# Four copies of the sums, a last block of one pair of bins per step, and a bias taken as a maximum, in a graph kernel

## The chip, the cores and the metric

The kernel runs on one core of a Trainium2 chip. Its time is that of one execution on the device, in microseconds (us), as the median of several runs. The core has five engines with a queue of instructions each, which run in order and wait for each other by semaphores: TensorE (PE in the rows; PEld is its weight load), VectorE (DVE), ScalarE (ACT), GpSimd (POOL) and SyncE (SP, which here only issues DMAs). Sixteen DMA engines move the data.

## The reference, cut to what matters

N = 6250 nodes of 64 values, E = 206250 edges sorted by `dst`, 64 values per edge:

```python
h = jnp.maximum(_layernorm(x), 0.0)                    # per node
m = jnp.concatenate([h[dst], edge_attr], axis=1)       # per edge
m = jax.nn.relu(m @ W1.T + b1)                         # 128 wide
m = jax.nn.relu(m @ W2.T + b2)                         # 128 wide
agg = segment_sum(m, src) / jnp.maximum(cnt, 1.0)      # by source node
z = jax.nn.relu(concatenate([h, agg, u[0]]) @ Wa.T + ba)
out = x + z @ Wb.T + bb
```

The edges come in the order of `dst`, the sums go by `src`, which lies at random. Everything is float32.

## The kernel before, in words

The edges are cut into 403 groups of 512 (four tiles of 128). The main loop has one step per group, and each engine runs the same steps from its own program; in step s PE works on group s in the first layer, on s-1 in the second and on s-2 in the sums.

The first layer of a group is one matmul (L1168) of 128x512: 64 rows are edge values, 64 select the projected node (`R`, built on DVE at L955 from the row `dstR` that SP broadcasts, and `L`, a window of the node table). ACT applies Relu (L821). The second layer is four matmuls (L1183) on top of one bf16 matmul (L1181) that puts b2 into the bank; ACT's Relu (L828) writes `h2`.

There are two ways to add a group's rows up by source. In a *plain* group (226 of them) DVE builds four masks of equal sources (L986), PE adds rows of the same source (L1157), ACT copies the result (L814), and POOL adds it to `sums` in memory by four indirect DMAs (L732). There are three copies of `sums` (NSETS), taken in turn; within one copy a scatter waits until the one before has landed. ACT's copy has four buffers, and waits for the landings of the group four plain ones before.

In a *sorted* group (177: the odd ones from 3 to 379, without every 24th from 95 on) DVE ranks the edges within 49 bins of source (L962, L964, L967), PE permutes the rows into slots, four per bin and 32 spare ones (L1133, two tiles ahead of the second layer and two behind), ACT copies them (L804), and SP stores them (L519). The spare ones are read back (L525), added by source with a mask (L974, PE L1194, ACT `vscat` L837, whose result also waits for an earlier landing) and scattered by POOL once (L720). The slots are collected by blocks of 30 sorted groups: for each of 25 pairs of bins, a *unit*, SP reads the block's rows (L536), DVE builds masks (L1016), PE adds (L1144, eight matmuls, 16 passes in the records), and DVE adds to `acc` in SBUF (L943). The reads have two buffers: unit m waits for unit m-2. Units of a block are spread over the steps of the next block; those of the last block, after the last sorted group, come two per step in steps 387 to 399, one behind the first layer and one at the step's end.

After the loop 13 chunks of rows follow: SP reads three copies, DVE adds them and `acc` (L1030 to L1032), divides by the count (L1035, L1036, L1039), PE transposes and applies the two last layers, and SP stores.

The order of work on an engine is only the order of the code in its `step`. Steps 0 to 4 of SP also write the zeros of the third copy (ZAFTER).

Of the kernel before, what the change touches and what calls it, by code (L numbers as in the profile page):

```python
# [5 lines left out]
P = 128  # L6
TILE = 128
# [22 lines left out]
NSETS = 3  # L30
ZQ = 5
ZFIRST, ZMID = 9, 2
ZAFTER = (0, 1, 1, 1, 1)
# [14 lines left out]
LAST_SORTED = 380  # L48
SKIP_FROM, SKIP = 72, 24
# [8 lines left out]
BLOCK = 30  # L58
# [11 lines left out]
def is_sorted(g):  # L70
    return 2 < g < LAST_SORTED and g % 2 == 1 and not (g >= SKIP_FROM and g % SKIP == SKIP - 1)

# [49 lines left out]
def mid_unit(s):  # L122
    return UNITS_AT[s][:-1] if s in UNITS_AT else []


def end_unit(s):
    return UNITS_AT[s][-1:] if s in UNITS_AT else []
# [12 lines left out]
assert NBIN == BA * BA and PACK * BA <= P and NS % (4 * PACK) == 0 and max(len(u) for u in UNITS_AT.values()) <= 2  # L140


def build(nc, x, src_cols, dst_cols, src_rows, dst_rows, ea, u, w1t, b1, w2t, b2, wat, ba, wbt, bb, out):
# [13 lines left out]
    with ctx:  # L157
# [64 lines left out]
        s1 = take(KC)  # L222
# [72 lines left out]
        rc = sb("rc", [P, 2, RCH], f32)  # L295
# [5 lines left out]
        psVsum = bank[:, 7, 2 * W:2 * W + C]  # L301
# [257 lines left out]
        def _(pool):  # L559
# [64 lines left out]
            whole(G.tensor_copy(b2p[:, 0, :], b2b[:, :]))  # L624
            whole(G.tensor_tensor(b2w[:, 0, :], b2b[:, :], b2p[:, 0, :], ALU.subtract))
            whole(G.tensor_copy(b2p[:, 1, :], b2w[:, 0, :]))
            whole(G.tensor_tensor(b2w[:, 1, :], b2w[:, 0, :], b2p[:, 1, :], ALU.subtract))
            whole(G.tensor_copy(b2p[:, 2, :], b2w[:, 1, :]))
            for k in range(3):
                whole(G.tensor_scalar(b2w[:, k % 2, :] if k < 2 else b2b[:, :], b2p[:, k, :], ident[:, k:k + 1], None, ALU.mult))  # L630
            whole(G.tensor_tensor(b2w[:, 0, :], b2w[:, 0, :], b2w[:, 1, :], ALU.add))
            whole(G.tensor_tensor(b2w[:, 0, :], b2w[:, 0, :], b2b[:, :], ALU.add))
            G.tensor_copy(b2R[:, :, :], b2w[:, 0, :].unsqueeze(1).broadcast_to([P, TPG, H])).then_inc(b2_ready, 1)
# [115 lines left out]
        def _(act):  # L749
# [46 lines left out]
            def evac_slots(g, t):  # L796

                n = BINNED_NO[g]
                act.wait_ge(slot_done, TPG * n + t + 1)
                if t == 3 and is_sorted(g + 2 - VSUM):  # L800
                    act.wait_ge(vsum_done, BINNED_NO[g + 2 - VSUM] + 1)
                if t == 0:
                    wait(act, slot_out[n % 2], 32 * (n // 2))
                nc.scalar.activation(slot_sb[:, n % 2, :, t, :], psSlot(t), ACT.Copy).then_inc(slot_ready, 1)  # L804

            for s in range(STEPS):
                g = s - 2
# [10 lines left out]
                if s < NG:  # L818
                    act.wait_ge(l1_done, s + 1)
                    wait(act, l2_done, s - 1)  # L820
                    nc.scalar.activation(h1[:, s % 2, :], psL1(s % 2), ACT.Relu).then_inc(h1_ready, 1)  # L821
                g = s - 1
                if 0 <= g < NG:
                    summed(act, g - 2)
                    if is_sorted(g):
                        nc.scalar.activation(h2[:, g % 2, :, C], srcF[:, TPG * g:TPG * (g + 1)], ACT.Copy).then_inc(key_ready, 1)
                    act.wait_ge(l2_done, g + 1)
                    nc.scalar.activation(h2[:, g % 2, :, 0:H], psL2(g % 2).rearrange("p (t f) -> p t f", t=TPG), ACT.Relu).then_inc(h2_ready, 1)  # L828
                if is_sorted(s - 2):
                    evac_slots(s - 2, 2)  # L830
                    evac_slots(s - 2, 3)
                if is_sorted(s - VSUM):
                    n = BINNED_NO[s - VSUM]
                    act.wait_ge(vsum_done, n + 1)
                    if n >= 2:
                        landed(act, BINNED[n - 2], 0)
                    nc.scalar.activation(vscat[:, n % 2, :], psVsum, ACT.Copy).then_inc(vscat_ready, 1)  # L837

            for c in range(NCH + 2):
                if c < NCH:  # L840
                    act.wait_ge(aggT_psum, c + 1)
# [4 lines left out]
                    nc.scalar.activation(aggT[:, c % 2, 0:w], bank[:, c % 2, 0:w], ACT.Copy).then_inc(aggT_ready, 1)  # L846
# [10 lines left out]
        def _(dve):  # L857
# [69 lines left out]
            dve.wait_ge(toscrap_ready, 1)  # L927
            dve.wait_ge(binF_ready, 1)
# [16 lines left out]
            for s in range(-3, STEPS + 1):  # L945
# [73 lines left out]
                if s == XBB_STEP:  # L1019
                    dve.wait_ge(wz_in, 16 * 8)  # L1020
# [3 lines left out]
            for c in range(NCH + 3):  # L1024
                if c < NCH:
# [4 lines left out]
                    link(VE.tensor_tensor(s1[:, 0:m * C], SA[:, s, 0, 0:m * C], SA[:, s, 1, 0:m * C], ALU.add))  # L1030
                    link(VE.tensor_tensor(s2[:, 0:m * C], s1[:, 0:m * C], SA[:, s, 2, 0:m * C], ALU.add))
# [3 lines left out]
                    link(VE.tensor_scalar(rc[:, 0, 0:m], s1v[:, :, H], 1.0, None, ALU.max))  # L1035
# [3 lines left out]
                    VE.tensor_tensor(agg[:, c % 2, 0:m, :], s1v[:, :, 0:H], rc[:, 1, 0:m].unsqueeze(2).broadcast_to([P, m, H]), ALU.mult).then_inc(agg_ready, 1)  # L1039
# [10 lines left out]
        def _(pe):  # L1050
# [58 lines left out]
            def free_last(s):  # L1109

                wait(pe, vscat_ready, sum(1 for g in BINNED if g <= s - VSUM - 1))

            def bin_tile(g, t, general):

                n = BINNED_NO[g]
                if t == 0:
# [5 lines left out]
                    free_last(g + 2)  # L1122
# [25 lines left out]
            def step(s, general):  # L1148
                g = s - 2
                if is_plain(g):  # L1150
                    n = PLAIN_NO[g]
                    pe.wait_ge(h2_ready, g + 1)
                    pe.wait_ge(mask_ready, n + 1)
                    free_sums(g - 1)
                    free_last(s)
                    for t in range(TPG):
                        last = T.matmul(bank[:, 6 + t // 2, (t % 2) * C:(t % 2 + 1) * C], S[:, n % 4, t, :], h2[:, g % 2, t, 0:C], start=True, stop=True)  # L1157
                    last.then_inc(sum_done, 1)
                if is_sorted(g):
                    bin_tile(g, 0, general)  # L1160
                    bin_tile(g, 1, general)
# [13 lines left out]
                for k, q in mid_unit(s):  # L1175
                    add_up(k, q, general)
                g = s - 1
                if 0 <= g < NG:
                    pe.wait_ge(h1_ready, g + 1)
                    wait(pe, h2_ready, g - 1)  # L1180
                    T.matmul(psL2(g % 2), onesb[:, :], b2R[:, :, :].rearrange("p t f -> p (t f)"), start=True, stop=False)  # L1181
                    for t in range(TPG):
                        last = T.matmul(psL2(g % 2)[:, t * H:(t + 1) * H], h1[:, g % 2, t * TILE:(t + 1) * TILE], w2[:, :], start=False, stop=t == TPG - 1)  # L1183
# [4 lines left out]
                if is_sorted(s - VSUM):  # L1188
                    n = BINNED_NO[s - VSUM]
                    pe.wait_ge(vmask_ready, n + 1)  # L1190
                    if not is_sorted(s - 2):
                        free_sums(min(s - 2, NG - 1))
                        free_last(s)
                    T.matmul(psVsum, vS[:, n % 2, :] if not general else zeros[:, 0:P], V[:, n % 2, 0:C], start=True, stop=True).then_inc(vsum_done, 1)  # L1194
# [19 lines left out]
                for k, q in end_unit(s):  # L1214
# [93 lines left out]
```

## Time and profile before

| | us |
|---|---|
| median of 3 runs (lowest, highest) | 2417.41 (2416.22, 2422.64) |
| profiled execution | 2404.49 |
| its span, first to last instruction | 2402.7 |
| busy: PE, DVE, ACT, POOL | 1894.7, 1289.1, 954.8, 1764.7 |
| mean granted clock of TensorE | 0.934 of full |
| DMA moved | 395.44 MB, 165 GB/s on average |

The profile is of one execution. Busy shares are averages over stages with different limits. A row of waits tells how long an engine stood idle before a line, and which event ended it; "issue" means that nothing in the profile was waited for. The chain of waits is followed back from the last instruction.

### The profile page before, as it was taken

What the parts mean: (1) busy time and instruction counts of PE and PEld (TensorE: products, weight loads), DVE (VectorE), ACT (ScalarE), POOL (GpSimd) and SP (SyncE); (2) the same over time, 40 slices, a digit from 0 to 9 for tenths busy, and PEclk for the clock granted to TensorE, in tenths of its full rate; (3) what the DMA queues carried; (4) which work ended last, traced back from release to release, by engine and by line L of the source; (5) the groups of instructions that cost most, each with busy time, mean ns of one, the idle gap of its engine ahead of it and who ended that gap; (6) DMA issues with size and microseconds to landing.
All of it is one profiled execution on the core that took longest, in us unless ns stands there. A gap on an engine that the chain in (4) does not pass through costs nothing.

```text
span 2402.7 us, 44999 instructions
## 1 busy us (share of the span) xinstructions
PE 1894.7 (79%) x12635; PEld 1565.7 (65%) x12840; DVE 1289.1 (54%) x4867; ACT 954.8 (40%) x2147; POOL 1764.7 (73%) x1131
## 2 busy tenths in 40 slices
PE   3788888888888888888888888888888879754546
PEld 2566666767766676767676677767677767553544
DVE  8655545555555555646555555555555656423227
ACT  2355544444434443444443444444443434311112
POOL 8477887777787777778777778787777777774370
PEclk8899999999999999999999999999999999876788
DMA  7688888988888888988888888988888889764446
GB/s 286 151 159 164 160 147 176 179 184 166 178 156 175 170 174 170 179 162 167 173 183 170 169 167 166 182 170 170 172 177 167 176 176 179 145 101 96 88 65 191
DMA packets 392057, 395.44 MB, mean 165 GB/s; under 512 B 51262, under 2 KB 296158, under 8 KB 391302
## 3 DMA queue, kind: packets, MB, share of 16 engines
q1 hardware_dynamic: 235030, 319.95, 48.3%
q0 software_dynamic: 155664, 71.47, 33.2%
q8 instruction: 113, 1.85, 0.3%
q10 hardware_dynamic: 1120, 1.11, 0.2%
q14 instruction: 130, 1.06, 0.2%
HBM read 221.11 MB, written 171.21 MB: 163 GB/s over the span
## 4 chain that ended last, share of the span: by engine, by line
POOL 33%; DMA 31%; issue 16%; PE 13%; DVE 4%; SPq 1%; ACT 1%; POOLq 0%; DVEq 0%; ACTq 0%
POOL sums L732 28%; DMA sums<-regA,idx 20%; DMA sums<-vscat,vidx 9%; POOL sums L720 4%; PE bank L1144 4%; PE bank L1183 3%; PE bank L1168 2%; PE bank L1157 2%; PE bank L1133 2%; DMA src<-rows_src 1%; DMA regC<-slots 1%; ACT h L828 1%; DVE regC L906 1%; DVE regC L986 1%; DVE regC L912 0%
## 5 line engine op out<-in xcount | busy, mean ns | idle before, releaser
L732 POOL DMA_INDIRECT sums<-regA,idx x904 | 1430.5, 1582 | 494.9 <-issue 232.5
L1183 PEld LDWEIGHTS bank<-w,h 128*128 128x128 f32 x3224 | 442.0, 199 | 151.4 <-issue 138.4
L1133 PE MATMUL bank<-h,regC 128*128 128x130 f32 x2832 | 397.4, 284 | 128.8 <-ACT h L828 128.8
L1133 PEld LDWEIGHTS bank<-h,regC 128*128 128x128 f32 x2832 | 352.6, 195 | 151.6 <-ACT h L828 151.6
L1183 PE MATMUL bank<-w,h 128*128 128x128 f32 x3224 | 439.7, 281 | 14.0 <-issue 4.2
L1168 PE MATMUL bank<-regA,L 128*128 128x512 f32 x806 | 435.4, 624 | 2.0 <-DVE regA L955 2.0
L1157 PE MATMUL bank<-h,regC 128*128 128x129 f32 x1808 | 260.0, 288 | 165.8 <-ACT vscat L837 135.0
L1144 PE MATMUL bank<-regC 120*128 120x129 f32 (+1 forms) x2352 | 314.6, 290 | 92.7 <-DVE regB L943 92.7
L828 ACT ACTIVATE h<-bank 128x512 f32<-128x512 f32 x403 | 241.1, 598 | 330.2 <-PE bank L1183 328.3
L804 ACT ACTIVATE regC<-bank 128x260 f32<-128x260 f32 x708 | 272.7, 386 | 244.3 <-PE bank L1133 187.5
L1144 PEld LDWEIGHTS bank<-regC 120*128 120x128 f32 (+1 forms) x2352 | 294.4, 203 | 104.1 <-issue 102.6
L1157 PEld LDWEIGHTS bank<-h,regC 128*128 128x128 f32 x1808 | 226.4, 196 | 200.3 <-issue 170.1
L720 POOL DMA_INDIRECT sums<-vscat,vidx x177 | 280.0, 1582 | 76.7 <-issue 43.6
L962 DVE TENSOR_REDUCE rank<-bank 128x4 f32<-128x196 f32 x177 | 64.1, 362 | 498.9 <-PE bank L1207 497.6
L814 ACT ACTIVATE regA<-bank 128x516 f32<-128x516 f32 x226 | 135.6, 600 | 492.3 <-PE bank L1157 245.1
L821 ACT ACTIVATE h<-bank 128x512 f32<-128x512 f32 x403 | 240.4, 597 | 151.7 <-PE bank L1168 150.4
L986 DVE SCALAR_TENSOR_TENSOR regC<-src,srcF,tri 128x128 f32<-128x128 uint16 x904 | 266.3, 350 | 18.1 <-DMA src<-rows_src 11.6
L1016 DVE SCALAR_TENSOR_TENSOR regC<-regC,lows 120x512 f32<-120x512 f32 (+1 forms) x294 | 189.8, 686 | 89.9 <-DMA regC<-slots 89.6
L955 DVE TENSOR_SCALAR regA<-dstR,oh_row 64x512 f32<-64x512 bf16 x403 | 205.5, 510 | 29.6 <-DMA dstR<-rows_dst 17.4
L949 DVE TENSOR_TENSOR regC<-bank,overs 128x128 f32<-128x128 f32 x177 | 51.5, 291 | 295.7 <-PE bank L1213 291.2
L964 DVE TENSOR_TENSOR regC<-bank,ranks 128x784 f32<-128x784 f32 x177 | 172.4, 974 | 5.6
L1168 PEld LDWEIGHTS bank<-regA,L 128*128 128x128 f32 x806 | 127.5, 199 | 3.1 <-DVE regA L955 2.9
(140 smaller groups left out, 1339.2 us busy)
## 6 DMA issues: line engine op xcount, KB each, us to landing
regC<-slots SPq DMA_DIRECT2D x245, 243.8 KB
regA<-in_ea SPq DMA_DIRECT2D x202, 256.0 KB
slots<-regC SPq DMA_DIRECT2D x177, 260.0 KB
slots<-regC SPq DMA_DIRECT2D x177, 203.1 KB
src<-rows_src SPq DMA_DIRECT2D x226, 128.0 KB
dstR<-rows_dst SPq DMA_DIRECT2D x403, 64.0 KB
sums<-regA,idx POOLq DMA_INDIRECT x904
L<-p_table SPq DMA_DIRECT2D x403, 32.0 KB
```

What stands on the lines that cost most here:

```text
L720: nc.gpsimd.indirect_dma_start(out=sums[k], out_offset=bass.IndirectOffsetOnAxis(ap=vidx[:, n % 4:n % 4 + 1], axis=0), in_=vscat[:, n % 2, ...
L732: nc.gpsimd.indirect_dma_start(out=sums[k], out_offset=bass.IndirectOffsetOnAxis(ap=idx[:, n % RING, t:t + 1], axis=0), in_=scat[:, n % 4, ...
L804: nc.scalar.activation(slot_sb[:, n % 2, :, t, :], psSlot(t), ACT.Copy).then_inc(slot_ready, 1)
L821: nc.scalar.activation(h1[:, s % 2, :], psL1(s % 2), ACT.Relu).then_inc(h1_ready, 1)
L828: nc.scalar.activation(h2[:, g % 2, :, 0:H], psL2(g % 2).rearrange("p (t f) -> p t f", t=TPG), ACT.Relu).then_inc(h2_ready, 1)
L955: VE.tensor_scalar(R[D:P, g % RING, :], dB[D:P, g % 4, :], oh_row[D:P, :], None, ALU.is_equal).then_inc(oh_ready, 1)
L986: mask = VE.scalar_tensor_tensor(out=S[:, n % 4, t, :], in0=sB[:, n % 4, t * TILE:(t + 1) * TILE], scalar=srcF[:, TPG * g + t:TPG * g + t ...
L1133: last = T.matmul(psSlot(t)[:, k, :], place, h2[:, g % 2, t, :], start=True, stop=True)
L1144: last = T.matmul(psUnit[:, i * C:(i + 1) * C], oh2[0:rows, m % 2, i, t, :] if not general else zeros[0:rows, 0:LO], BR[0:rows, m % UNIT_R ...
L1157: last = T.matmul(bank[:, 6 + t // 2, (t % 2) * C:(t % 2 + 1) * C], S[:, n % 4, t, :], h2[:, g % 2, t, 0:C], start=True, stop=True)
L1168: T.matmul(psL1(s % 2), L[:, s % RING, :], R[:, s % RING, :], start=True, stop=True).then_inc(l1_done, 1)
L1183: last = T.matmul(psL2(g % 2)[:, t * H:(t + 1) * H], h1[:, g % 2, t * TILE:(t + 1) * TILE], w2[:, :], start=False, stop=t == TPG - 1)
```

## The change

There are four copies of `sums`, so that a scatter waits for the landing of the fourth before it; the zeros of the fourth copy are written in steps 5 to 7 of SP. All odd groups from 3 to 367 are sorted (183), none is skipped, and groups 368 to 402 are all plain; blocks have 31 sorted groups. Units come in even steps, at most one per step, always at the end of PE's step; those of the last block one per step in steps 376 to 400. PE and ACT do the first layer ahead of the sums. The second layer's matmul of b2 is gone: DVE writes max(W2 h1, -b2) into `h2`, which is relu(W2 h1 + b2) - b2, and b2 is added behind the mean, in ACT's evacuation of the transposed mean (with Relu, and a term that keeps nodes without edges at 0). POOL only negates b2. The sum of the spare slots moves from bank 7 to bank 1 (that of the units) and behind the ranks in PE's step, so `free_last` goes.

```diff
-NSETS = 3
+NSETS = 4
-ZAFTER = (0, 1, 1, 1, 1)
+ZAFTER = (0, 1, 1, 1, 1, 1, 2, 2)
-LAST_SORTED = 380
-SKIP_FROM, SKIP = 72, 24
+LAST_SORTED = 368
-BLOCK = 30
+BLOCK = 31
 def unit_steps():
-    firsts = [block[-1] + VREAD + 1 for block in BLOCKS]
+    firsts = [block[-1] + VREAD + 2 for block in BLOCKS]
...
-            s = firsts[k] + (firsts[k + 1] - firsts[k]) * q // UNITS if k + 1 < len(BLOCKS) else firsts[k] + q // 2
+            s = firsts[k] + 2 * ((firsts[k + 1] - firsts[k]) * q // (2 * UNITS)) if k + 1 < len(BLOCKS) else firsts[k] + q
...
-        psVsum = bank[:, 7, 2 * W:2 * W + C]
+        psVsum = bank[:, 1, PAIR * C:(PAIR + 1) * C]
...
 ACT, step s
+                if s < NG:
+                    act.wait_ge(l1_done, s + 1)
+                    wait(act, l2_done, s - 1)
+                    nc.scalar.activation(h1[:, s % 2, :], psL1(s % 2), ACT.Relu).then_inc(h1_ready, 1)
                 g = s - 2
...
-                    act.wait_ge(l2_done, g + 1)
-                    nc.scalar.activation(h2[:, g % 2, :, 0:H], psL2(g % 2)..., ACT.Relu).then_inc(h2_ready, 1)
...
 DVE, step s
-                for k, q in end_unit(s - 1) + mid_unit(s):
+                for k, q in UNITS_AT.get(s - 1, ()):
                     add_unit(k, q)
+                g = s - 1
+                if 0 <= g < NG:
+                    dve.wait_ge(l2_done, g + 1)
+                    summed(dve, g - 2)
+                    VE.tensor_tensor(h2[:, g % 2, :, 0:H], psL2(g % 2)..., b2n[:, :]..., ALU.max).then_inc(h2_ready, 1)
...
 DVE, chunks at the end
-                    link(VE.tensor_tensor(s1[:, 0:m * C], SA[:, s, 0, 0:m * C], SA[:, s, 1, 0:m * C], ALU.add))
-                    link(VE.tensor_tensor(s2[:, 0:m * C], s1[:, 0:m * C], SA[:, s, 2, 0:m * C], ALU.add))
+                    link(VE.tensor_tensor(s1[:, :, 0:m * C], SA[:, s, 0:2, 0:m * C], SA[:, s, 2:4, 0:m * C], ALU.add))
+                    link(VE.tensor_tensor(s2[:, 0:m * C], s1[:, 0, 0:m * C], s1[:, 1, 0:m * C], ALU.add))
...
+                    VE.tensor_scalar(rc[:, 2, 0:m], s1v[:, :, H], 0.5, None, ALU.is_lt)
...
-                    VE.tensor_tensor(agg[:, c % 2, 0:m, :], s1v[:, :, 0:H], rc[:, 1, 0:m]..., ALU.mult).then_inc(agg_ready, 1)
+                    for r in range(m):
+                        made = VE.tensor_scalar(agg[:, c % 2, r, :], s1v[:, r, 0:H], rc[:, 2, r:r + 1], rc[:, 1, r:r + 1], ALU.add, ALU.mult)
...
 PE, step s
-                    T.matmul(psL2(g % 2), onesb[:, :], b2R[:, :, :].rearrange("p t f -> p (t f)"), start=True, stop=False)
...
+                if is_sorted(s - VSUM):
+                    n = BINNED_NO[s - VSUM]
+                    pe.wait_ge(vmask_ready, n + 1)
+                    wait(pe, vscat_ready, n)
+                    wait(pe, acc_ready, units_until(s - 1))
+                    T.matmul(psVsum, ...)
+                for k, q in UNITS_AT.get(s, ()):
+                    wait(pe, vscat_ready, sum(1 for g in BINNED if g <= s - VSUM))
                     add_up(k, q, general)
```

How the order moves is seen in three places. In the rows L and a number is the line of the program itself, so the same operation has another number after the change.

PE before, an odd step in the main stretch (`h,regC` bins, `regA,L` first layer, `b2R,onesb` bias, `w,h` second layer, `V` spare slots, `A` ranks), up to the next step's plain sums:

```order
L1133 MATMUL bank<-h,regC 128x130 x4
L1168 MATMUL bank<-regA,L 128x512
L1181 MATMUL bank<-b2R,onesb 128x512
L1183 MATMUL bank<-w,h 128x128 x4
L1133 MATMUL bank<-h,regC 128x130 x4
L1194 MATMUL bank<-V,vS 128x129
L1200 MATMUL bank<-ident,V 128x128
L1207 MATMUL bank<-A,prefix 128x196
L1157 MATMUL bank<-h,regC 128x129 x4
```

The same step after the change:

```order
L1140 MATMUL bank<-regA,L 128x512
L1118 MATMUL bank<-h,regC 128x130 x4
L1164 MATMUL bank<-w,h 128x128 x4
L1118 MATMUL bank<-h,regC 128x130 x4
L1174 MATMUL bank<-ident,V 128x128
L1181 MATMUL bank<-A,prefix 128x196
L1193 MATMUL bank<-V,vS 128x129
L1140 MATMUL bank<-regA,L 128x512
L1154 MATMUL bank<-h,regC 128x129 x4
```

The first layer has moved ahead of the bins, the bias is gone, and the sum of the spare slots stands last.

DVE before, from the end of an even step through an odd one into the next (`vextra`, `vidx` the spare slots' index; `regC,lows` a unit's masks; `regA` the first layer's R):

```order
L1003 SCALAR_TENSOR_TENSOR vextra<-vcnt,scrapc 128x1
L1007 TENSOR_TENSOR vidx<-vextra,V 128x1
L1016 SCALAR_TENSOR_TENSOR regC<-regC,lows 120x512 x2
L949 TENSOR_TENSOR regC<-bank,overs 128x4x32
L955 TENSOR_SCALAR regA<-dstR,oh_row 64x512
L986 SCALAR_TENSOR_TENSOR regC,cnt<-src,srcF,tri 128x128 x4
L999 TENSOR_TENSOR idx<-extra,srcF 128x4
L955 TENSOR_SCALAR regA<-dstR,oh_row 64x512
L962 TENSOR_REDUCE rank<-bank 128x4
```

The same stretch of DVE after the change (`h<-bank,b2n` is the maximum):

```order
L986 SCALAR_TENSOR_TENSOR vextra<-vcnt,scrapc 128x1
L990 TENSOR_TENSOR vidx<-vextra,V 128x1
L997 TENSOR_TENSOR h<-bank,b2n 128x4x128
L932 TENSOR_TENSOR regC<-bank,overs 128x4x32
L938 TENSOR_SCALAR regA<-dstR,oh_row 64x512
L969 SCALAR_TENSOR_TENSOR regC,cnt<-src,srcF,tri 128x128 x4
L982 TENSOR_TENSOR idx<-extra,srcF 128x4
L926 TENSOR_TENSOR regB<-regB,bank 128x258
L997 TENSOR_TENSOR h<-bank,b2n 128x4x128
L1004 SCALAR_TENSOR_TENSOR regC<-regC,lows 124x512 x2
L938 TENSOR_SCALAR regA<-dstR,oh_row 64x512
L945 TENSOR_REDUCE rank<-bank 128x4
```

The maximum stands near the end of each step, behind the index or the masks and the unit's add, and ahead of the next unit's masks.

PE before, one step of the last block (`regC` alone is a unit):

```order
L1157 MATMUL bank<-h,regC 128x129 x4
L1168 MATMUL bank<-regA,L 128x512
L1144 MATMUL bank<-regC 128x129 x8
L1181 MATMUL bank<-b2R,onesb 128x512
L1183 MATMUL bank<-w,h 128x128 x4
L1144 MATMUL bank<-regC 128x129 x8
```

And after the change:

```order
L1140 MATMUL bank<-regA,L 128x512
L1154 MATMUL bank<-h,regC 128x129 x4
L1164 MATMUL bank<-w,h 128x128 x4
L1129 MATMUL bank<-regC 128x129 x8
L1140 MATMUL bank<-regA,L 128x512
```

One unit, at the end, takes the place of two on either side of the second layer.

## Rows read from the trace of the kernel before

**Rows 1.** Page, part 1: busy us (share of the span) and instructions.

```profile
PE 1894.7 (79%) x12635; PEld 1565.7 (65%) x12840; DVE 1289.1 (54%) x4867; ACT 954.8 (40%) x2147; POOL 1764.7 (73%) x1131
```

**Rows 2.** Waits: engine, line <- releaser: us in total, times, longest us.

```profile
DVE rank L962 <- PE bank L1207: 497.6, 175, 10.6
...
POOL sums L732 <- DMA sums<-regA,idx: 142.6, 164, 2.9
...
PE bank L1157 <- ACT vscat L837: 135.0, 126, 4.7
...
POOL sums L732 <- ACT regA L814: 81.7, 13, 9.9
...
POOL sums L732 <- DMA sums<-vscat,vidx: 35.0, 38, 1.9
...
POOL sums L720 <- DMA sums<-regA,idx: 28.5, 27, 2.5
```

**Rows 3.** Groups: line engine op out<-in xcount | busy us, mean ns | idle before.

```profile
L732 POOL DMA_INDIRECT sums<-regA,idx x904 | 1430.5, 1582 | 494.9 <-issue 232.5 <-DMA sums<-regA,idx 142.6 <-ACT regA L814 81.7
...
L720 POOL DMA_INDIRECT sums<-vscat,vidx x177 | 280.0, 1582 | 76.7 <-issue 43.6 <-DMA sums<-regA,idx 28.5 <-DVE idx L999 2.4
...
L828 ACT ACTIVATE h<-bank 128x512 f32<-128x512 f32 x403 | 241.1, 598 | 330.2 <-PE bank L1183 328.3 <-issue 1.8
...
L1181 PE MATMUL bank<-b2R,onesb 128*128 128x512 bf16 x198 | 77.9, 394 | 0.0
...
L902 DVE TENSOR_TENSOR regB<-bank,b1b 128x512 f32<-128x512 f32 x12 | 9.1, 759 | 2.2 <-PE bank L1073 2.1
...
L1039 DVE TENSOR_TENSOR regC<-regC,rc 128x512 f32<-128x512 f32 x12 | 8.3, 692 | 0.7 <-DVE rc L1036 0.3
...
L1035 DVE TENSOR_SCALAR rc<-regC 128x4 f32<-128x4 f32 x12 | 2.0, 170 | 0.4
```

**Rows 4.** Windows: from:to length, busy (xcount) by engine, PEclk, DMA share, GB/s.

```profile
100.00:400.00 300.00, 251.37 (x1672) 200.10 (x1704) 159.99 (x680) 154.04 (x357) 240.06 (x154) 0.99 0.87 160
400.00:2000.00 1600.00, 1352.18 (x9303) 1125.41 (x9451) 890.64 (x3500) 689.26 (x1586) 1243.24 (x784) 0.97 0.87 172
2125.00:2295.00 170.00, 85.94 (x492) 78.62 (x502) 51.82 (x170) 17.60 (x30) 81.52 (x51) 0.70 0.51 94
```

**Rows 5.** Chain of waits near 1007 us: start us, us, what.

```profile
1007.73 5.85 DMA sums<-regA,idx
1013.58 0.27 issue
1013.85 1.54 POOL sums L732
```

**Rows 6.** Timeline of POOL: its first and its last scatter.

```profile
88.32 1.76 POOL L732 DMA_INDIRECT sums<-regA,idx  x1 [25.89 <-issue]
...
2343.04 1.54 POOL L732 DMA_INDIRECT sums<-regA,idx  x1 [0.30 <-issue]
```

**Rows 7.** Chain of waits, one step of the last block.

```profile
2179.79 0.87 PE bank L1168 x2
...
2182.34 0.59 SPq L506
2182.97 3.69 DMA src<-rows_src
...
2188.53 3.78 PE bank L1144 x16
...
2193.89 1.79 PE bank L1144 x16
...
2205.64 3.78 PE bank L1144 x16
```

**Rows 8.** Waits of SP over the span.

```profile
SPq L536 <- PE bank L1144: 140.0, 24, 23.1
```

**Rows 9.** Windows of 10 us, the one from 1150.

```profile
1150.00:1160.00 10.00, 9.46 (x72) 8.08 (x71) 6.40 (x24) 4.72 (x12) 8.48 (x6) 1.00 0.86 170
```

More of the change, by code:

```diff
@@ L70, in is_sorted @@
 def is_sorted(g):
-    return 2 < g < LAST_SORTED and g % 2 == 1 and not (g >= SKIP_FROM and g % SKIP == SKIP - 1)
+    return 2 < g < LAST_SORTED and g % 2 == 1
 def is_plain(g):
@@ L119, with units_until @@
 UNIT_NO = {kq: n for n, kq in enumerate(kq for s in sorted(UNITS_AT) for kq in UNITS_AT[s])}
[L122 to L127, printed above, removed]
+def units_until(s):
+    return sum(len(u) for at, u in UNITS_AT.items() if at <= s)
 def arrived(m):
@@ L623, in _ @@
             pool.wait_ge(b2_in, 16)
[L624 to L633, printed above, removed]
+            G.tensor_scalar(b2n[:, :], b2b[:, :], -1.0, None, ALU.mult).then_inc(b2_ready, 1)
             pool.wait_ge(mode_ready, 1)
@@ L845, in _ @@
                     w = (r1 - r0) * P
-                    nc.scalar.activation(aggT[:, c % 2, 0:w], bank[:, c % 2, 0:w], ACT.Copy).then_inc(aggT_ready, 1)
+                    nc.scalar.activation(aggT[:, c % 2, 0:w], bank[:, c % 2, 0:w], ACT.Relu, bias=b2c[:, :]).then_inc(aggT_ready, 1)
                 if 1 <= c <= NCH:
@@ L1148, in step @@
             def step(s, general):
[L1149 to L1161, printed above, removed]
                 if s < NG:
@@ L1174, in step @@
                         last.then_inc(l1_done, 1)
-                for k, q in mid_unit(s):
-                    add_up(k, q, general)
+                g = s - 2
+                if is_plain(g):
+                    n = PLAIN_NO[g]
+                    pe.wait_ge(h2_ready, g + 1)
+                    pe.wait_ge(mask_ready, n + 1)
+                    free_sums(g - 1)
+                    for t in range(TPG):
+                        last = T.matmul(bank[:, 6 + t // 2, (t % 2) * C:(t % 2 + 1) * C], S[:, n % 4, t, :], h2[:, g % 2, t, 0:C], start=True, stop=True)
+                    last.then_inc(sum_done, 1)
+                if is_sorted(g):
+                    bin_tile(g, 0, general)
+                    bin_tile(g, 1, general)
                 g = s - 1
@@ L1180, in step @@
                     wait(pe, h2_ready, g - 1)
[L1181 removed]
                     for t in range(TPG):
[L1183 removed]
+                        last = T.matmul(psL2(g % 2)[:, t * H:(t + 1) * H], h1[:, g % 2, t * TILE:(t + 1) * TILE], w2[:, :], start=True, stop=True)
                     last.then_inc(l2_done, 1)
@@ L1187, in step @@
                     bin_tile(s - 2, 3, general)
[L1188 to L1194, printed above, removed]
                 if is_sorted(s - VBC):
@@ L1213, in step @@
                     T.matmul(psOver, prefix[:, :], over[:, n % 2, :], start=True, stop=True).then_inc(over_done, 1)
-                for k, q in end_unit(s):
+                if is_sorted(s - VSUM):
[3 more added lines that the diff above has]
+                    wait(pe, acc_ready, units_until(s - 1))
+                    T.matmul(psVsum, vS[:, n % 2, :] if not general else zeros[:, 0:P], V[:, n % 2, 0:C], start=True, stop=True).then_inc(vsum_done, 1)
+                for k, q in UNITS_AT.get(s, ()):
+                    wait(pe, vscat_ready, sum(1 for g in BINNED if g <= s - VSUM))
                     add_up(k, q, general)
```

39 lines of the change are left out of this document (15 added, 24 removed).

## The prediction

> **What bounds the kernel now.** I read the busy times first, then the list of waits, then the costliest groups, then windows of the main stretch, and last the chain of waits at its end. The busy times [rows 1] name no bound: PE 79%, POOL 73%, and PE's share is made of stages. The waits do. POOL issues 904 + 177 = 1081 scatters (indirect DMAs that add 128 rows each into a copy of `sums`), 1582 ns each [rows 3]. Between two of them 0.30 us pass even when nothing is waited for; 1.54 + 0.30 is the step between back-to-back ones, and with the mean of 1.58 a scatter costs POOL at least 1.88 us. From the first scatter at 88.32 to the end of the last at 2343.04 + 1.54 = 2344.58 [rows 6] are 2256.3 us. 1081 x 1.882 = 2034.4 of these are POOL's own work; 222 us are waits. The list of waits splits them [rows 2]: behind the landing of an earlier scatter 142.6 + 35.0 + 28.5 = 206.1 us in 229 waits, less 0.30 each that would have passed anyway, is 137 us; behind ACT's copy L814 81.7 us in 13 waits, less 4, is 78 us; the rest is 7.
>
> The 137 us are the three copies. Scatter n may only start when scatter n-3 has landed. In the chain a scatter started at 1007.73 holds it until landing at 1013.58, and the next starts at 1013.85 [rows 5]: 5.85 us, where three steps take 3 x 1.85 = 5.55. Through the buffers of ACT this reaches PE, which waits 135 us at L1157 for the copy of `vscat` [rows 2]; that copy waits for a landing.
>
> The 78 us are the end of the main stretch. After step 386 two pairs of bins are added per step. From 2125 to 2295 only 51 scatters start in 170 us, 3.3 us each, at a granted clock of 0.70 and a DMA share of 0.51 [rows 4]: no engine is full. The chain there [rows 7] is a loop: last pair of bins (L1144, 16 passes) ends; SP, which waited for it (140 us at L536, [rows 8]), reads the row number (L501), issues `dstR` and `src` for the next step, 3.69 us until landing; VectorE's masks; then the first pair, 3.78 us; second layer; second pair. 2188.53 to 2205.64, from a first pair to the next, is 17.1 us per step, of which POOL can use 4 x 1.88 = 7.5.
>
> **The change, part by part.** *Fewer scatters.* Sorted groups go from 177 to 183 and plain ones from 226 to 220: each swap takes 3 scatters, so 1063 remain: 1063 x 1.882 = 2000.6 us, 34 less.
>
> *Fourth copy.* Now scatter n-4 must have landed, and 4 x 1.85 = 7.4 us cover it. At today's load 229 of 1081 waited, by under 3 us; most would be gone. But faster scatters load the DMA engines more. Before pairs of bins are read (100 to 400 us) five scatters (a couple of groups, one plain and one sorted) take 300 / 154 x 5 = 9.74 us at a DMA share of 0.87; with them (400 to 2000) 1600 / 784 x 5 = 10.20 us, again at 0.87 [rows 4]. So a couple needs 8.5 and 8.9 us of all 16 engines. At POOL's floor of 5 x 1.882 = 9.41 the second would be a share of 0.94, which no long window shows. Bounds: nothing left (0 us) if the share goes to 0.94; all 137 us stay if 0.87 is the most. With one more scatter in flight I take 0.91, that is 9.76 us, 0.07 us per scatter more than the floor on some 740 scatters: 52 us stay. The set's five zero writes come in steps 5 to 7, and the fourth scatter waits for them: I add 3 us of at most 10.
>
> The Trainium skill ("DMA: Bandwidth & Descriptors", section "Anatomy of one DMA — SWDGE (gpsimd) path") fits a GpSimd DMA with 2.0 us plus bytes over 436 GB/s. By that estimate a scatter of 66 KB has landed after 2.15 us, three copies never wait, and the fourth brings nothing: the time would be that of the second rival below. The chain's 5.85 us disagrees, so the sum goes by the row.
>
> *Last block one pair per step.* With the last sorted group at 367, units run in steps 376 to 400, one each. The loop by rows: unit m is read when unit m-2 is done, now two steps back. SP about 2 us for the reads, 3 us for row number and loads of the next step, landing 3.69, masks and add 2, L1144 1.79 to 3.78 [rows 7]: 12.5 to 14.5 us for two steps, 6.2 to 7.2 a step, just under POOL's 7.53 for a plain group. So POOL bounds the end: the 78 us go, and I leave 10 us for it being so close. The order of PE shows both pairs around the second layer before, one at the end now.
>
> *Bias as a maximum.* PE loses one bf16 matmul of 512 columns per group, 394 ns each in the records [rows 3]. It is not on the chain (POOL is): 0 us. PE was busy 1352 / 1600 x 10.20 = 8.6 us per couple [rows 4], now 7.8 to 8.2 of 9.76. ACT gives up L828, 598 ns; VectorE takes a 128x512 operation out of PSUM, between 598 ns (ACT's) and 759 ns (L902, PSUM plus a broadcast row [rows 3]): 0.70. VectorE goes from 891 / 1600 x 10.20 = 5.7 to 7.1 us of 9.76, 73%. What counts is order: VectorE does it after this step's rank or mask work, and PE needs it for the sums of the next step. In between PE has the pair of bins (1.79) or two bin tiles, and now also the first layer (0.87 [rows 7]), since that moved ahead of the sums: some 2.6 us of cover for 0.7 us. VectorE starts its step when PE's step before ends, does up to 3.3 us, and PE's first layer, sums and second layer take 2.7: it is late by 0.6 at most. I take it as hidden, 0 us. It gains nothing by itself, since ACT is not on the path; without the cover it costs what the fourth rival says. ACT's wait for a landing now comes after the first layer's Relu, which helps.
>
> *psVsum in bank 1.* PE waits for the last unit's add and the last `vscat` copy. Both lie over half a step back: 0. GpSimd's splitting of b2 before the loop ends well ahead of the spill test; start unchanged.
>
> *End.* 2402.70 - 2344.58 = 58.1 us. Twelve full chunks on VectorE each: the first add is twice as wide (+0.54, bounds 0.5 to 0.7), one more small operation (0.17 [rows 3], mostly overlapped), `agg` as four operations instead of one of 0.69: bounds -0.4 and +0.4, take +0.1. 0.75 x 12 = 9 us: 67.1.
>
> **Sum.** 88.3 + 2000.6 + 3 + 52 + 10 + 67.1 = 2221 us span. The profiled execution took 2404.49 with a span of 2402.70: + 1.8 = 2223. The median of the runs, 2417.41, is 0.54% above the profiled one: 2235 us.
>
> **Rivals.**
> *1, better:* the DMA engines follow and nothing is left of waits: 2223 - 65 = 2158, as a median 2170. For it: windows of 10 us in which POOL has no gap beyond the 0.30 (8.48 us busy, [rows 9]) at a share of 0.86; against: 0.94 share over 1500 us.
> *2, DMA is full:* share stays at 0.87, the fourth scatter in flight only waits longer. Then all 137 us remain: 2223 + 85 = 2308, median 2320. For it: 0.87 in both stretches of different load.
> *3, the end stays a loop:* one pair per step still costs 10 us (clock at 0.70, L1144 3.78 us, SP in between), 25 x (10 - 7.5) = 62, less the 10: 2275, median 2287. For it: loop and POOL differ by under 1 us.
> *4, slower:* VectorE is in order, and the second layer's result now stands behind waits for PE (L962 waits 498 us for L1207 [rows 2]). If PE then waits for VectorE in each step, both run in turns. Place: PE's L1154 and L1118 waiting for L997. Price: 183 couples; slower than before begins where a couple takes (2417 - 2235) / 183 = 1.0 us over 9.76. Doing VectorE's 7.1 us with only 6 of PE's 8 beside it, 9.1, does not get there; with the full step of each 4.4 + 1.3 twice it is 11.4 and the time 2535.
> *5, no change in effect:* gains and losses cancel within 0.3%.
>
> **Chances.** Forecast 0.47; rival 1 0.13; rival 2 0.20; rival 3 0.12; rival 4 0.06; rival 5 0.02. Faster by over 0.3% (what a measurement of this kernel can tell) 0.92, same 0.02, slower 0.06. The range reaches from under rival 1 (2150) to over rival 2 (2345) and leaves out rivals 4 and 5 and a little of the ends.
>
> **What would show it.** Right: POOL's waits for landings under 70 us; five scatters in 9.6 to 9.9 us and a DMA share of 0.90 or more from 400 us on; no 17 us steps after the last sorted group, but POOL without gaps for 35 plain groups; L997 at about 0.7 us and PE hardly waiting for it; chunks of 4.4 us at the end. Wrong: landings of over 7.4 us at a share of 0.87 (rival 2); gaps in POOL after step 376 behind L1129 (3); PE idle behind L997 (4).

## The result, and the profile after

The changed kernel takes 4458.4 us (median of 4 runs, 4456.53 to 4460.27), the kernel before 2416.81 beside it: a ratio of 1.844, interval 1.841 to 1.848. The forecast was 2235.

The busy times of the changed kernel (page, part 1; they answer to [rows 1]) are much the same work in nearly twice the time:

```profile
PE 2048.0 (46%) x12521; PEld 1756.7 (39%) x12521; DVE 1568.4 (35%) x5313; ACT 737.3 (17%) x1774; POOL 1684.0 (38%) x1103
```

Its windows (from:to, length, busy us and count of PE, PEld, DVE, ACT, POOL, then granted clock, DMA share, GB/s) tell where the time lies, and answer to [rows 4]:

```profile
100.00:380.00 280.00, 234.37 (x1546) 194.39 (x1545) 191.18 (x721) 105.84 (x277) 234.00 (x151) 0.94 0.88 163
800.00:1600.00 800.00, 323.48 (x2008) 282.15 (x2008) 237.33 (x815) 116.17 (x288) 253.58 (x164) 0.69 0.37 78
...
4200.00:4300.00 100.00, 71.87 (x454) 61.44 (x452) 55.20 (x202) 14.59 (x26) 83.86 (x54) 0.88 0.81 146
```

Up to 380 us POOL starts 151 scatters in 280 us, 1.85 us each: its floor, where three copies gave 1.95. Before units are read, the fourth copy frees POOL, as forecast. In the middle a scatter takes 800 / 164 = 4.9 us, five of them 24 us, and every engine and the DMA engines are idle most of the time. From 4200 us on the floor is back.

The waits (engine, line <- releaser: us, times, longest) name what appeared:

```profile
ACT h L794 <- PE bank L1140: 2984.9, 328, 28.8
POOL sums L705 <- ACT vscat L818: 2293.6, 120, 23.5
DVE regC L1004 <- DMA regC<-slots: 2181.9, 137, 23.7
PEld bank L1187 <- DVE over L950: 2172.3, 122, 24.2
PE bank L1187 <- DVE vS L957: 2152.6, 122, 24.1
```

L1004 builds a unit's masks and waits for the unit's read. POOL's own waits for landings, 206 us in [rows 2], come to 2.0 us in 3 waits here. PE's weight load waits for L997 at most 1.3 us at a time. By form (line engine op out<-in xcount | busy, mean ns | idle before), the 124 rows of a block of 31 groups have 2157.9 us of the wait, and the last block, 28 groups or 112 rows, has 25.2:

```profile
L1004 DVE SCALAR_TENSOR_TENSOR regC<-regC,lows 124x512 f32<-124x512 f32 x245 | 158.6, 688 | 2157.9 <-DMA regC<-slots 2157.9
...
L1004 DVE SCALAR_TENSOR_TENSOR regC<-regC,lows 112x512 f32<-112x512 f32 x49 | 31.7, 687 | 25.2 <-DMA regC<-slots 24.0 <-PE bank L1129 1.2
```

The chain of waits (start us, us, what), which answers to [rows 5], is a loop of 30 us. A unit has two reads; SP issues the second at 998.38, and both have landed 24.42 us later (in stretches of the chain of the kernel with blocks of 30, below, such a piece takes 4.8 to 6.1 us). Then come the masks, the unit, and the next read. SP's own issues are long in it too, 4.66 and 11.61 us for one DMA, and the store of slots that follows takes 10.10 us to land:

```profile
998.38 24.42 DMA regC<-slots
...
1026.68 3.52 PE bank L1129 x16
...
1035.52 4.66 SPq L530
...
1041.45 11.61 SPq L496
...
1054.82 10.10 DMA slots<-regC
```

125 units in blocks of 31 between the first read at 386 us and some 4140 us are 30 us each. Two reads of 124 rows, 2080 bytes each, in 24.4 us are 98 ns per row. That is near the pace of one DMA engine: by the page of the kernel before, its queues took 82% of 16 engines x 2402.7 us for 392057 packets, 81 ns per packet of 1009 bytes on average.

Windows of 1 us while the two reads are out and POOL issues nothing (columns as above) show it directly:

```profile
1005.00:1006.00 1.00, 1.00 (x12) 1.00 (x11) 0.49 (x1) 0.05 (x2) 0.00 (x0) 1.00 0.06 25
1006.00:1007.00 1.00, 1.00 (x10) 0.94 (x9) 0.20 (x1) 0.78 (x3) 0.00 (x0) 1.00 0.06 25
```

A DMA share of 0.06 is one engine of 16. The Trainium skill states a rule that fits this ("DMA: Bandwidth & Descriptors", section "Why a DMA increments its semaphore by 16 and not by 1"): a DMA runs on the largest number of engines up to 16 that divides the slowest dimension of source and destination. Here these are 31 groups and 124 partitions, so 1; before, 30 and 120, so 15. The trace agrees for 31, with its share of 0.06; no view names the engines of one DMA, so the other counts below are counts by the rule.

### The profile page after: what moved, and what is told of

Same layout as the page of the kernel before. It is cut to its first block, busy times and chain, and to the rows that moved or that the text cites. A ratio compares the mean times of both kernels' runs of the same rounds, so it can differ in the third digit from the quotient of the medians.

```text
span 4458.5 us, 44483 instructions
## 1 busy us (share of the span) xinstructions
PE 2048.0 (46%) x12521; PEld 1756.7 (39%) x12521; DVE 1568.4 (35%) x5313; ACT 737.3 (17%) x1774; POOL 1684.0 (38%) x1103
## 4 chain that ended last, share of the span: by engine, by line
DMA 39%; SPq 37%; PE 8%; POOL 7%; issue 6%; DVE 3%; ACT 0%; DVEq 0%; POOLq 0%; ACTq 0%
DMA slots<-regC 23%; SPq L496 22%; DMA regC<-slots 14%; SPq L530 9%; POOL sums L717 6%; PE bank L1129 2%; SPq L500 2%; SPq L495 2%; PE bank L1118 2%; SPq L513 1%; PE bank L1140 1%; PE bank L1164 1%; DMA sums<-regA,idx 1%; SPq L519 1%; POOL sums L705 1%
## 5 line engine op out<-in xcount | busy, mean ns | idle before, releaser
L717 POOL DMA_INDIRECT sums<-regA,idx x880 | 1368.6, 1555 | 322.3 <-issue 261.1
L1187 PE MATMUL bank<-over,prefix 128*128 128x4 bf16 x183 | 30.3, 165 | 2152.7 <-DVE vS L957 2152.6
L1004 DVE SCALAR_TENSOR_TENSOR regC<-regC,lows 124x512 f32<-124x512 f32 (+1 forms) x294 | 190.3, 688 | 2183.1 <-DMA regC<-slots 2181.9
L1187 PEld LDWEIGHTS bank<-over,prefix 128*128 128x128 bf16 x183 | 18.8, 103 | 2172.8 <-DVE over L950 2172.3
L794 ACT ACTIVATE h<-bank 128x512 f32<-128x512 f32 x403 | 240.7, 597 | 2988.2 <-PE bank L1140 2984.9
L1129 PE MATMUL bank<-regC 124*128 124x129 f32 (+1 forms) x2352 | 513.6, 406 | 39.5 <-issue 37.6
L1129 PEld LDWEIGHTS bank<-regC 124*128 124x128 f32 (+1 forms) x2352 | 481.3, 312 | 44.1 <-issue 39.9
L1140 PE MATMUL bank<-regA,L 128*128 128x512 f32 x806 | 468.0, 665 | 2.2 <-DVE regA L938 2.0
L1118 PEld LDWEIGHTS bank<-h,regC 128*128 128x128 f32 x2928 | 389.6, 201 | 173.1 <-issue 147.4
L997 DVE TENSOR_TENSOR h<-bank,b2n 128x512 f32<-128x512 f32 x403 | 278.7, 692 | 469.8 <-PE bank L1164 441.1
L1164 PEld LDWEIGHTS bank<-w,h 128*128 128x128 f32 x3224 | 412.5, 200 | 1.1 <-ACT h L794 0.6
L1154 PEld LDWEIGHTS bank<-h,regC 128*128 128x128 f32 x1760 | 238.3, 198 | 177.1 <-issue 173.5
```

The lines of the kernel that those rows point to most:

```text
L717: nc.gpsimd.indirect_dma_start(out=sums[k], out_offset=bass.IndirectOffsetOnAxis(ap=idx[:, n % RING, t:t + 1], axis=0), in_=scat[:, n % 4, ...
L997: VE.tensor_tensor(h2[:, g % 2, :, 0:H], psL2(g % 2).rearrange("p (t f) -> p t f", t=TPG), b2n[:, :].unsqueeze(1).broadcast_to([P, TPG, H] ...
L1118: last = T.matmul(psSlot(t)[:, k, :], place, h2[:, g % 2, t, :], start=True, stop=True)
L1129: last = T.matmul(psUnit[:, i * C:(i + 1) * C], oh2[0:rows, m % 2, i, t, :] if not general else zeros[0:rows, 0:LO], BR[0:rows, m % UNIT_R ...
L1140: T.matmul(psL1(s % 2), L[:, s % RING, :], R[:, s % RING, :], start=True, stop=True).then_inc(l1_done, 1)
```

## The experiments

Twelve kernels ran, on three chips. Each ratio is to the kernel before on the same chip, with its 95% interval. The kernel before took 2407 to 2421 us on the three, so kernels on different chips are compared by their ratios where a few us matter (0.01 is 24 us).

**Blocks of 30.**

```diff
-LAST_SORTED = 368
-BLOCK = 31
+LAST_SORTED = 362
+BLOCK = 30
```

> The changed kernel with blocks of 30 sorted groups in place of 31, and so 180 sorted groups (the last is 361) in place of 183. Theory A (a read of a unit takes one row range of each group of the block, and with 31 of them, a prime, all of it runs on one DMA engine, while 30 spread over 15): the 30 us per unit go, and the time is the sum of the prediction with 9 scatters more, 2150 to 2320 us, best guess 2220; the waits of VectorE's unit masks for their read fall from 2182 us to under 100. Theory B (VectorE in order with the second layer's maximum behind its waits, the prediction's fourth rival): nothing of that changes, over 4000 us.

Measured: 2253.03 us, 0.934 (0.930 to 0.937). Smaller blocks and three sorted groups fewer halve the time, and VectorE's masks wait 88 us for their reads in place of 2182. The rows of POOL's waits, and two windows:

```profile
POOL sums L717 <- issue: 263.9, 866, 0.3
POOL sums L705 <- ACT vscat L818: 79.6, 50, 3.6
POOL sums L717 <- DVE idx L982: 49.1, 5, 47.9
POOL sums L705 <- issue: 40.1, 127, 0.7
POOL sums L717 <- DMA sums<-zeros: 6.0, 1, 6.0
```

```profile
400.00:2000.00 1600.00, 1404.47 (x9826) 1201.82 (x9826) 1147.82 (x4022) 551.04 (x1355) 1287.07 (x812) 0.96 0.92 185
2000.00:2100.00 100.00, 68.81 (x398) 57.39 (x396) 49.40 (x189) 14.48 (x26) 83.85 (x54) 0.85 0.83 144
```

POOL has not one wait for the landing of a scatter left (only one of 6.0 us for the zeros), and the last block runs at 1.85 us per scatter where [rows 4] had 3.3.

**Blocks of 32, 32 and four of 30.**

```diff
-LAST_SORTED = 368
-BLOCK = 31
+LAST_SORTED = 370
+SIZES = (32, 32, 30, 30, 30, 30)
```

> The changed kernel with blocks of 32, 32, 30, 30, 30 and 30 sorted groups (184, the last is 369). Theory A: 32 spreads over 16 engines; within 1% of the kernel with blocks of 30, a little faster for 12 scatters less (22 us). A third theory, C (the reads are slow because they come to over 120 partitions, not because 31 can't be divided): slow in its first two blocks of 32, 50 units of 30 us in place of some 11 to 12, about 900 us more than with blocks of 30. Theory B: over 4000 us.

Measured: 2201.46 us, 0.912 (0.909 to 0.915). Theory C falls: masks of 128 rows wait 2.0 us in 98 operations. It beats blocks of 30 by 52 us, where 12 scatters are 22; this is 2.3%, more than the 1% expected.

**The same block of 31, each read in two.**

```diff
-    sp.dma_start(BR[0:CAP * len(block), ...], slots[h0:h0 + len(block), ...])
+    for c0, c1 in ((0, 16), (16, 31)):
+        sp.dma_start(BR[CAP * c0:CAP * c1, ...], slots[h0 + c0:h0 + c1, ...])
```

> The changed kernel with its blocks of 31 and everything else, but each read of a block of 31 cut into two DMAs, of 16 and of 15 groups: the same bytes, rows and places. Theory A: 16 and 15 engines, the time falls to 2150 to 2350 us; SP issues two more DMAs per unit of two bins (about 2 us for 125 units, which it may not all hide). Theories B and C: over 4000 us.

Measured: 2376.96 us, 0.986 (0.982 to 0.990). The same bytes to the same places save 2081 us. That shows theory A by itself: what was slow is the shape of one DMA. It stayed above the range expected. VectorE now waits 246 us for the load of `dstR` (129 with blocks of 30), and SP's four issues per unit take 3.1 us together (1.9 for two with blocks of 30). That points at SP's queue as the cost of the split; no run tests it.

**The kernel before, with blocks of 31.**

```diff
-BLOCK = 30
+BLOCK = 31
```

> The kernel before with blocks of 31 sorted groups in place of 30 (five of 31, one of 22), nothing else changed. Theory A: 125 units of 30 us as in the changed kernel, from about 390 us on: 4200 to 4500 us. Theory B: the size of a block is not the cause, so 2417 us within 2%. Theory C: as A.

Measured: 4291.79 us, 1.779 (1.773 to 1.784). The row of its masks, by form:

```profile
L1016 DVE SCALAR_TENSOR_TENSOR regC<-regC,lows 124x512 f32<-124x512 f32 x245 | 158.7, 688 | 2325.4 <-DMA regC<-slots 2325.4
```

The one number alone makes the old kernel as slow: nothing of the new order or of VectorE is needed for it.

**Mixed block sizes.**

```diff
 (the kernel with blocks of 32, 32 and four of 30)
-LAST_SORTED = 370
-SIZES = (32, 32, 30, 30, 30, 30)
+LAST_SORTED = 338
+SIZES = (32, 25, 26, 28, 27, 30)
```

> One look: the changed kernel with blocks of 32, 25, 26, 28, 27 and 30 sorted groups (168, the last is 335), so that one trace holds reads that would run on 16, 5, 13, 14, 9 and 15 DMA engines by the largest number up to 16 that divides the block. Theory A in numbers, from 12 us per read of 124 rows on one engine (0.1 us per row): a read of 25 groups (100 rows) on 5 engines lands some 2 to 4 us after its issue, so VectorE waits for it longer than in the blocks of 26, 28 and 32, and a couple of groups takes longest there. Theory C (the number of rows decides): the blocks of 25 and 26 are alike and the fastest.

Measured: 2321.38 us in one run. The idle time of VectorE before the masks, by form (rows = 4 x groups, 49 operations each):

```profile
L1004 DVE SCALAR_TENSOR_TENSOR regC<-regC,lows 108x512 f32<-108x512 f32 x49 | 31.9, 690 | 16.7 <-DMA regC<-slots 16.6
L1004 DVE SCALAR_TENSOR_TENSOR regC<-regC,lows 104x512 f32<-104x512 f32 x49 | 31.8, 689 | 13.3 <-DMA regC<-slots 12.6 <-issue 0.6
L1004 DVE SCALAR_TENSOR_TENSOR regC<-regC,lows 100x512 f32<-100x512 f32 x49 | 31.7, 687 | 28.5 <-DMA regC<-slots 28.4
L1004 DVE SCALAR_TENSOR_TENSOR regC<-regC,lows 112x512 f32<-112x512 f32 x49 | 31.7, 687 | 11.8 <-DMA regC<-slots 11.2 <-issue 0.3
...
L1004 DVE SCALAR_TENSOR_TENSOR regC<-regC,lows 128x512 f32<-128x512 f32 x49 | 31.4, 682 | 0.0
```

By engines, counted by the rule: 16 (32 groups) 0.0 us, 14 (28) 11.8, 13 (26) 13.3, 9 (27) 16.7, 5 (25) 28.5, and 1 (31, from the changed kernel) 2157.9 / 5 = 432 per 49. Within this kernel the order is that of the engines, not of the rows: 25 groups are the fewest rows and wait longest. The block of 30 (17.1 us) is the last one, with a unit in each step, and doesn't compare; before the last block, the kernel with blocks of 30 has 59.8 us in 234 masks, 12.5 per 49, no less than 28 groups have here with one engine fewer. And the first block of 28 in the kernel with four blocks of 32, next, has 6.4 per 49. So from 14 engines up the count does not order the waits by itself; what came before counts too. Nor was the expectation on the pace borne out: a scatter took 1.89 us while blocks of 32 were read, 2.02 with 25, 2.02 with 26, 1.98 with 28 and 1.94 with 27 (windows of 200 to 250 us).

**Four blocks of 32.**

```diff
-SIZES = (32, 32, 30, 30, 30, 30)
+SIZES = (32, 32, 32, 32, 28, 28)
```

> The changed kernel with blocks of 32, 32, 32, 32, 28 and 28 sorted groups (184 in all, the last is 369, as in the kernel with two blocks of 32). While units of a block of 32 were read there, POOL ran at its floor of 1.88 us per scatter, at a DMA share of 0.97; with blocks of 30 it took 1.95 at 0.93. If that is the engines that a read spreads over (16 against 15), the two further blocks of 32 bring 0.06 us on some 300 scatters, 18 us, less what 28 (14 engines) loses: 2185 us. If it is the place in the program (less backlog later), nothing: 2201.

Measured: 2172.47 us, 0.898 (0.894 to 0.903), a gain of 29 us (32 by the ratios) where 16 were expected. But it does not lie where the expectation put it. From 1000 to 1540 us, while blocks of 32 are read, POOL starts 284 scatters here and 278 in the kernel with two blocks of 32 (blocks of 30 by then), which is 11 us. From 1540 to 2000, while the first block of 28 is read, it starts 242 and 233, another 17 us, where the 14 engines of the rule were to lose. Windows of 400 to 1000 us, in which two blocks of 30 are read in the first kernel and blocks of 32 in the second (the one with two of them), show what 32 is worth against 30 early in the loop:

```profile
400.00:1000.00 600.00, 532.82 (x3762) 455.59 (x3762) 435.91 (x1518) 215.69 (x539) 486.34 (x307) 0.97 0.93 188
```

```profile
400.00:1000.00 600.00, 550.04 (x3977) 472.78 (x3976) 461.25 (x1612) 216.98 (x571) 503.10 (x319) 0.98 0.97 202
```

1.95 against 1.88 us per scatter. With 30 groups VectorE waits for reads, 26.5 us in this window, and PE 58.9 us behind it; with 32 it is 2.0 and 14.1. What makes the read of 32 the better one is not shown. SP's two issues for a unit take 1.22 us with 32 groups and 1.66 to 1.89 with 25, 26, 27, 28 and 30, so the time of issue is a rival to 16 engines against 15, and no run parts them. With four blocks of 32 POOL does not wait behind `vscat` in the blocks of 28 either, although their masks still wait 25.4 us in 98 operations, 19 of them in the last block.

**Three copies** in the kernel with two blocks of 32:

```diff
-NSETS = 4
+NSETS = 3
... (the zeros, and three copies read at the end)
```

> The kernel with blocks of 32, 32 and four of 30, with three copies of the sums in place of four (the chunks at the end read three). If landings of three copies hold POOL as in the kernel before (137 us of waits), 2201 + 137 - 9 at the end - 7 for zeros, 2320 us, with POOL's waits for landings back at over 100 us. If the new order alone freed POOL, no more than 2210.

Measured: 2276.66 us, 0.941 (0.937 to 0.947): the fourth copy is worth 3.0%, 71 us, less than the 119 expected. The waits come back:

```profile
POOL sums L717 <- DMA sums<-regA,idx: 123.2, 152, 2.0
...
POOL sums L705 <- DMA sums<-regA,idx: 46.9, 52, 2.5
POOL sums L717 <- DMA sums<-vscat,vidx: 28.8, 34, 2.5
```

They are 198.9 us in 238 waits, less 0.30 each, 128 us. Against them POOL's 42.2 us behind ACT's `vscat` in the kernel with four copies are gone, and so is the cost of the fourth copy that the expectation puts at 9 + 7 us. That leaves about 76.

**Bias back on PE, Relu on ACT**, in the same kernel:

```diff
+    T.matmul(psL2(g % 2), onesb[:, :], b2R..., start=True, stop=False)
...
-    VE.tensor_tensor(h2[...], psL2(g % 2)..., b2n..., ALU.max)
+    nc.scalar.activation(h2[...], psL2(g % 2)..., ACT.Relu)
```

> The kernel with blocks of 32, 32 and four of 30, with the second layer's bias put back: one bf16 matmul of 512 columns per group on PE, Relu on ACT, no maximum on VectorE (b2 is then not added behind the mean). If the bias as a maximum is hidden, as predicted, 2201 us within 1%. If PE is now next to POOL, the 0.4 us per couple of groups show where POOL was kept waiting by PE: up to 40 us more. If VectorE with its maximum is what holds PE (102 us at the over matmul behind VectorE), it gets faster by up to 60 us.

Measured: 2201.61 us, 0.911 (0.907 to 0.915), against 2201.46 (0.912) without: no difference beyond the intervals, as forecast.

**The kernel before with a fourth copy:**

```diff
-NSETS = 3
+NSETS = 4
... (the zeros, and four copies read at the end)
```

> The kernel before with a fourth copy of the sums, nothing else changed (zeros of it written in steps 5 to 7, four copies read at the end). If three copies cost 137 us there, 2417 - 137 + 9 + 7, and some of it kept by the fuller DMA engines: 2290 to 2330 us. If the gain of the whole change comes from the order and not from the copies: 2417 within 1%.

Measured: 2285.49 us, 0.947 (0.942 to 0.951), a little more gained than expected. 784 scatters from 400 to 2000 us [rows 4] have become 847, 1.89 us each, and POOL's waits for landings 7.8 us in 18 waits (3.4, 2.6 and 1.8 by line). The wait behind ACT at the end (78 us in the prediction) is still there:

```profile
POOL sums L732 <- ACT regA L814: 72.9, 14, 9.9
```

**The kernel before with one unit per step at the end:**

```diff
-LAST_SORTED = 380
-BLOCK = 30
+LAST_SORTED = 368
+SIZES = (30, 30, 28, 28, 28, 27)
-    ... else firsts[k] + q // 2
+    ... else firsts[k] + q
```

> The kernel before with the last sorted group at 367 and one unit per step in the last block (blocks of 30, 30, 28, 28, 28, 27; 171 sorted groups), three copies and the old order. The wait of 78 us behind ACT at the end goes, 18 scatters more cost 34 us: 2417 - 78 + 34, 2375 us. If the loop stays with one unit per step (10 us a step), 2430 us.

Measured: 2374.47 us, 0.985 (0.982 to 0.989). The number is the one expected, but the kernel before took 2407 on this chip: by the ratio the gain is 35 us where 42 were expected. POOL waits 1.5 us behind ACT's L814 in place of 81.7. With the 34 us paid for 18 more scatters, 69 of the 78 us went. The blocks are smaller too, so one unit per step is not the only edit; masks of the last block (27 groups) wait 80.0 us, 83.6 in the kernel before.

**Blocks of 32 five times, and 28:**

```diff
 (the kernel with blocks of 32, 32 and four of 30)
-LAST_SORTED = 370
-SIZES = (32, 32, 30, 30, 30, 30)
+LAST_SORTED = 378
+SIZES = (32, 32, 32, 32, 32, 28)
```

> The changed kernel with blocks of 32 five times and 28 (188 sorted groups, the last is 377, units of the last block in steps 386 to 410, nine of them after the last group). 12 scatters fewer than with 184: 22 us, and POOL nearer its floor. Against it the units end later than the last scatter's group: 9 steps of a unit's loop, about 6 us each, less POOL's backlog of 20 us: 2150 to 2190 us.

Measured: 2144.03 us, 0.892 (0.889 to 0.894), the best of all, 10.8% under the kernel before and a little below the range expected. POOL is at its floor in the whole main stretch, 1600 / 849 = 1.885 us per scatter:

```profile
400.00:2000.00 1600.00, 1429.88 (x10221) 1228.17 (x10222) 1193.01 (x4187) 547.91 (x1427) 1341.57 (x849) 0.97 0.94 194
```

**The old order with the new copies and blocks:**

```diff
 (the kernel before)
-NSETS = 3
+NSETS = 4
-LAST_SORTED = 380
+LAST_SORTED = 370
-BLOCK = 30
+SIZES = (32, 32, 32, 32, 28, 28)
-    return 2 < g < LAST_SORTED and g % 2 == 1 and not (g >= SKIP_FROM and g % SKIP == SKIP - 1)
+    return 2 < g < LAST_SORTED and g % 2 == 1
-    ... else firsts[k] + q // 2
+    ... else firsts[k] + q
... (the zeros, and four copies read at the end)
```

> The kernel before (its order of work, its bias on PE and Relu on ACT, its units at any step) with the three other parts: four copies, 184 sorted groups without gaps in blocks of 32, 32, 32, 32, 28 and 28, and one unit per step in the last block. If order and bias are worth nothing, the 2172 us of the changed kernel with the same blocks; if the first layer first helps, 2190 to 2230 us; if the new order holds PE behind VectorE (143 us with blocks of 30), less than 2172.

Measured: 2180.07 us, 0.906 (0.904 to 0.908), against 0.898 (0.894 to 0.903) of the kernel with the same blocks and the new order. They ran on different chips: by the ratios the new order and the bias together are worth 0.8%, with intervals that all but touch, and by the medians (2180.07 against 2172.47) 0.35%. So a gain of the new order is likely, and not shown.

## Why the prediction was wrong

**The step that failed** is the term for the units in the main stretch. The sum charges them only as load, "a couple needs 8.5 and 8.9 us of all 16 engines", and so takes each unit's read as spread over the engines and landed in time, as with blocks of 30. No term at all stands for blocks of 31 in place of 30; the size was treated as bookkeeping. It put the read on one engine (a DMA share of 0.06): 24.4 us until a unit's two reads have landed, 30 us per unit, 125 units, some 2200 us in all (4458 against 2253). The last block, the only one whose loop the prediction adds up step by step, has 28 groups and was not hit. None of the five rivals held it. The forecast of the sign was wrong through this alone: the kernel with blocks of 30, the one with each read in two, and the kernel before with blocks of 31 show it from three sides.

**The rest of the sum, tested on the kernel with blocks of 30.** It has 1072 scatters where the sum has 1063; 9 x 1.88 more make the forecast 2252. Measured 2253. That they meet is in part luck. The forecast of the span is 2221 + 17 = 2238 us, and it was 2251.3, 13 us more; the 12 us that the prediction adds because the runs before had a median above the profiled one were not there (2253.03 against 2253.05). The terms behind that:

- POOL's floor: 1694 us busy and 0.30 for each of 1072, 2016; by the prediction's 1.882, 2018. Right.
- Waits left: from the first scatter at 87.77 to the end of the last at 2179.80 are 2092, so 76 against 65 forecast. The size was near by luck, the mechanism wrong: 52 of the 65 were to be waits for landings, and none is left. What is left are 79.6 us in 50 waits behind ACT's `vscat`, less 0.30 each, 65 us. By the lists of waits, reads that land late hold VectorE's masks (88.0 us), VectorE holds PE at L1187 (143.2), and PE holds ACT. With four blocks of 32 they are gone; whether by the count of engines or by the shorter issue is open.
- "At POOL's floor ... a share of 0.94, which no long window shows": 0.97 was reached for 600 us at the floor. Rival 2 (DMA full at 0.87) is false. Rival 1 had 2170 us, and the kernel with four blocks of 32, which has one sorted group more than the change, took 2172.
- The fourth copy: 137 us of waits. In the kernel before it brought 129 (0.053 of 2421), in the new order 71 (0.030 of 2417), each after its own cost.
- The end: 78 us to go and 10 to stay; with one unit per step in the kernel before 69 went. Right, and rival 3 with it false: 54 scatters in 100 us in the last block.
- The bias: 0 us, and none measured; L997 takes 690 ns, 700 were forecast. Rival 4 is false: with blocks of 30 PE and its weight load wait 47 us in all for L997, at most 1.7 us at a time.
- The end of the kernel: 2251.3 - 2179.8 = 71.5 us against 67.1.
- The set's zeros: one wait of 6.0 us, 3 forecast.

The estimate from the Trainium skill's fit (2.0 us plus bytes over bandwidth, "DMA: Bandwidth & Descriptors", section "Anatomy of one DMA — SWDGE (gpsimd) path"), by which the fourth copy brings nothing, is refuted by both runs on it: 129 and 71 us.

## What to carry to other kernels

A size that sets the outer dimension of a DMA is a cost of its own: before a block, tile or ring size is changed, work out into how many equal shares each DMA that it shapes can be cut, and look at the time per row of that DMA. 31 groups, which can't be cut into 2 to 16 equal shares, doubled the time. Blocks of 32 were worth some 30 to 57 us over blocks of 30 here, beyond the scatters that they save (by the ratios 53 - 22 and 102 - 45; the second kernel also moves the last block). And a list of parts is only complete when each changed constant has been followed to every instruction that it shapes, also the ones that look like bookkeeping.

A hit in the number says little about the terms behind it: 2252 against 2253 held a wait of the right size for the wrong reason.

## What the runs showed of the hardware

- Two DMAs of 124 rows of 2080 bytes in the shape 31 x 4 keep one of 16 engines busy (a share of 0.06) and take 24.4 us, 98 ns per row. With each cut into 16 and 15 groups the wait for them falls from 2158 to 88 us in 245 masks.
- While such a DMA is out, what SP issues behind it is late too: an issue of 0.5 us at the median took up to 16 us, and the store of slots landed after 10 us, where stretches of the chain with blocks of 30 have 4.7 to 5.0.
- Two reads of blocks of 32 groups are issued in 1.22 us, of 25 in 1.66, of 27 in 1.73, of 28 in 1.80, of 26 in 1.83 and of 30 in 1.89 us.
- All 16 DMA engines were busy 97% of 600 us while POOL waited 0.3 us in all for a landing, with four scatters in flight.
- From 800 to 1600 us of the changed kernel PE was busy 40% of the time, and the mean granted clock was 0.69 of full; from 100 to 380 us it was busy 84% and the clock 0.94. Windows of 1 us there have 0.50 or 1.00, the levels of 1.2 and 2.4 GHz, or a mean of both. At 0.50 a unit's 16 passes took 3.52 us, where [rows 7] have 1.79 us too.
